# New order lists for five engines in a graph-network kernel of four layers

## The reference

```python
H = (adj != 0); w = adj[:, 0]                       # layer 0: hypergraph convolution, twice
h = relu(Dn * (H @ (Be * (H.T @ (x @ W1.T)))) + b1) # Dn, Be: reciprocals of row sums
x = ln(x + conv(ln0(h), W2) + b2 + x)
q, k = split(x @ Wqk); v = x @ Wv                   # layer 1: a softmax over the nodes
x = ln(x + softmax(sum(q * (adj @ k)) / 16) * v)
s = (Q @ K.T) * scale * 2 * adj                     # layer 2: attention, 8 heads of 32
x = ln(x + (softmax(s) @ V) @ Wo.T + bo)
xg = x * sigmoid(deg * Wd + bd)                     # layer 3: gated, scores times adj
QK = sigmoid(xg @ Wqk3.T + bqk); a = (QK @ QK.T) * adj
x = ln(x + relu((a / sum(a)) @ xg @ Wl.T + bl + xg @ Wr.T))
```

## Time and profile before

| | us |
|---|---|
| runs before (three), median | 960.44 |
| lowest and highest | 959.28, 968.0 |
| span of the profiled execution | 966.0 |
| busy: TensorE | 887.1 (92%) |
| busy: VectorE, ScalarE, GpSimd | 742.3, 724.6, 670.3 |

### The profile page before, as it was taken

The page is one execution under the profiler, slowest core; times in us unless marked ns, Lnnn a source line. Parts: engine busy times, 40 slices in busy tenths (PEclk is TensorE's granted clock), DMA queues, the critical chain, the costliest instruction groups (busy, mean ns, idle before and its releaser), DMA issues.

```text
span 966.0 us, 34322 instructions
## 1 busy us (share of the span) xinstructions
PE 887.1 (92%) x12124; PEld 761.5 (79%) x12124; DVE 742.3 (77%) x2292; ACT 724.6 (75%) x1740; POOL 670.3 (69%) x1005
## 2 busy tenths in 40 slices
PE   4778898999999999999999999999999999988674
PEld 3556677888888888888888888888888888876542
DVE  5556776888888888888888888888888888876632
ACT  3445567888888888888888888888888888867631
POOL 2575667777777787777777777877778777764421
PEclk9798899999999999999999999999999999999955
DMA  8002443444454444444344444443443444444320
GB/s 207 20 21 83 111 100 65 119 111 106 112 123 121 116 116 102 103 112 109 106 109 110 122 123 117 114 106 99 111 119 103 104 115 116 109 97 116 97 48 22
DMA packets 194573, 99.46 MB, mean 103 GB/s; under 512 B 112866, under 2 KB 194276, under 8 KB 194532
## 3 DMA queue, kind: packets, MB, share of 16 engines
q1 hardware_dynamic: 194532, 98.93, 40.6%
HBM read 48.28 MB, written 25.17 MB: 76 GB/s over the span
## 4 chain that ended last, share of the span: by engine, by line
PE 53%; ACT 11%; POOL 10%; DVE 10%; issue 9%; DMA 5%; SPq 1%; POOLq 0%; DVEq 0%; ACTq 0%
PE bank L537 12%; PE bank L539 12%; PE bank L538 12%; POOL rFl L1375 3%; PE bank L562 3%; ACT r L886 3%; PE bank L754 2%; PE bank L815 2%; DMA k_by_head<-kst 2%; DMA Ks<-k_by_head 2%; PE bank L650 1%; ACT x L846 1%; PE bank L682 1%; ACT rFh L826 1%; POOL rsC L1391 1%
## 5 line engine op out<-in xcount | busy, mean ns | idle before, releaser
L1375 POOL TENSOR_TENSOR rFl<-r,rFh 128x512 f16<-128x512 f32 x64 | 74.2, 1160 | 81.1 <-ACT rFh L826 81.1
L537 PE MATMUL bank<-z1h,W 128*128 128x256 f16 x256 | 71.9, 281 | 6.3 <-DVE z1l L1025 6.3
L538 PE MATMUL bank<-z1l,W 128*128 128x256 f16 x256 | 71.8, 281 | 0.0
L537 PE MATMUL bank<-W,rFh 128*128 128x256 f16 x256 | 71.8, 280 | 0.0
L539 PE MATMUL bank<-z1h,W 128*128 128x256 f16 x256 | 71.7, 280 | 0.0
L539 PE MATMUL bank<-W,rFl 128*128 128x256 f16 x256 | 71.7, 280 | 0.0
L538 PE MATMUL bank<-W,rFh 128*128 128x256 f16 x256 | 71.7, 280 | 0.0
L1476 POOL TENSOR_TENSOR late<-late,Smx 128x512 f32<-128x512 f32 x64 | 66.8, 1043 | 1.3 <-DVE Smx L1282 1.0
L1375 POOL TENSOR_TENSOR y0l<-y,y0h 128x512 f16<-128x512 f32 x32 | 37.3, 1166 | 42.3 <-ACT y0h L826 42.3
L870 ACT ACTIVATE Pf<-bank,Dinv 128x128 f32<-128x128 f32 x64 | 20.0, 363 | 49.7 <-DVE Dinv L1167 49.7
L886 ACT ACTIVATE r<-bank,b1c 128x256 f32<-128x256 f32 x128 | 50.1, 471 | 4.8 <-PE bank L539 4.8
(11 more groups left out here) (281 smaller groups left out, 4188.3 us busy)
## 6 DMA issues: line engine op xcount, KB each, us to landing
Qs<-q_by_head SPq DMA_DIRECT2D x96, 128.0 KB, 2.7
Ks<-k_by_head SPq DMA_DIRECT2D x96, 128.0 KB, 3.2
Vbd<-vst SPq DMA_DIRECT2D x128, 66.0 KB, 2.1
xin<-x SPq DMA_DIRECT2D x32, 256.0 KB, 2.8
q_by_head<-qst SPq DMA_DIRECT2D x32, 256.0 KB, 2.5
k_by_head<-kst SPq DMA_DIRECT2D x32, 256.0 KB, 2.1
out<-late SPq DMA_DIRECT2D x32, 256.0 KB, 2.9
aC<-adj_mask SPq DMA_DIRECT2D x32, 65.0 KB, 2.2
```

Source lines behind the costliest of these rows:

```text
L537: pe.matmul(o, sh, mh, start=start, stop=False, skip_group_check=True)
L538: pe.matmul(o, sh, ml, start=False, stop=False, skip_group_check=True)
L1375: return pool.tensor_tensor(dst, a, b, ALU.subtract)
```

## The change

All order lists (`ORDER`, `HEAD` and `TAIL` for TensorE, ScalarE, VectorE, GpSimd and SP) are replaced; a step holds the same pieces, and nothing else of the kernel differs. The lists were drawn up by a planner that now counts the changes between whole-array and 64-wide products. Two of the fifteen tables:

```diff
-ORDER_PE = [3, 2, 1, 5, 2, 4, 4, 2, 0, 3, 1, 0, 2, 0, 5, 4, 0, 0, 5, 3, 1, 3, 4, 5, 1, 2, 5, 5, 2, 0, 1, 0, 4]
+ORDER_PE = [1, 2, 3, 3, 5, 0, 2, 1, 5, 0, 4, 4, 2, 0, 2, 4, 0, 1, 5, 3, 3, 0, 4, 5, 2, 1, 5, 5, 1, 2, 0, 0, 4]
-ORDER_ACT = [0, 4, 3, 2, 1, 0, 0, 3, 5, 0, 5, 2, 5, 1, 4, 0, 0, 0, 0, 1, 2, 0, 4, 5, 0, 3, 2, 4, 3, 4, 1, 4, 2, 3, 3, 4, 5]
+ORDER_ACT = [4, 1, 0, 3, 5, 5, 0, 0, 2, 5, 0, 1, 3, 4, 4, 2, 1, 4, 2, 0, 0, 0, 0, 5, 0, 2, 0, 1, 3, 4, 3, 4, 3, 2, 4, 3, 5]
```

More of the change, by code:

```diff
@@ L61 @@
-TAIL_POOL = [[1, 1, 3, 4, 5, 1, 1, 1, 3, 1, 2, 2, 3, 4, 4, 4, 5, 5, 5], [4, 3, 5, 2, 2, 4, 4, 3, 3, 4, 5, 5, 5], [4, 5, 4, 4, 3, 4, 3, 5, 3, 5, 5], [4, 5, 4, 4, 4, 5, 5, 5], [5, 5, 5, 5]]
+ORDER_PE = [1, 2, 3, 3, 5, 0, 2, 1, 5, 0, 4, 4, 2, 0, 2, 4, 0, 1, 5, 3, 3, 0, 4, 5, 2, 1, 5, 5, 1, 2, 0, 0, 4]
+ORDER_SP = [4, 3, 3, 0, 3, 0, 3, 0, 5, 2, 3, 2, 2]
+HEAD_SP = [[0, 0, 0], [0, 0, 0], [0, 0, 2, 0, 2, 2], [3, 0, 3, 3, 0, 3, 3, 2, 0, 2, 2], [3, 3, 0, 4, 0, 0, 3, 2, 3, 3, 2, 2], [3, 0, 3, 3, 0, 0, 3, 4, 2, 5, 3, 2, 2]]
@@ new lines @@
+TAIL_SP = [[3, 3, 4, 3, 3, 2, 5, 3, 2, 2], [3, 5, 4, 3, 3, 3, 2, 3, 2, 2], [3, 5, 3, 4, 3, 3, 3], [4, 5], [5]]
+ORDER_ACT = [4, 1, 0, 3, 5, 5, 0, 0, 2, 5, 0, 1, 3, 4, 4, 2, 1, 4, 2, 0, 0, 0, 0, 5, 0, 2, 0, 1, 3, 4, 3, 4, 3, 2, 4, 3, 5]
+ORDER_DVE = [1, 0, 0, 0, 2, 0, 0, 0, 2, 0, 3, 0, 0, 1, 1, 1, 0, 4, 4, 2, 2, 4, 5, 4, 0, 5, 2, 4, 3, 3, 5, 3, 1, 5, 3, 5, 3, 5, 4, 2, 1, 3, 3, 5, 1, 0, 1, 5, 5, 0, 2, 0, 4, 3]
+ORDER_POOL = [0, 0, 1, 1, 0, 3, 0, 4, 1, 1, 1, 2, 2, 1, 5, 3, 0, 0, 0, 4, 0, 4, 3, 4, 5, 5, 0, 5, 0]
@@ new lines @@
+HEAD_PE = [[0, 0, 0, 0, 0, 6, 6, 6, 0, 0], [1, 0, 0, 0, 1, 0, 0, 6, 1, 1, 0, 1, 0], [2, 1, 2, 2, 0, 2, 0, 1, 0, 0, 0, 1, 2, 1, 2, 1, 0, 0], [1, 2, 3, 2, 2, 0, 1, 0, 2, 0, 3, 0, 3, 3, 0, 2, 1, 1, 2, 1, 0, 0], [2, 1, 4, 3, 4, 0, 2, 4, 1, 2, 0, 4, 0, 2, 3, 0, 0, 3, 1, 4, 3, 2, 1, 2, 1, 0, 0], [1, 3, 2, 3, 5, 1, 2, 4, 4, 0, 2, 5, 0, 2, 4, 0, 1, 3, 3, 5, 0, 0, 1, 5, 2, 4, 5, 5, 1, 2, 0, 0, 4]]
+HEAD_ACT = [[6, 0, 0, 0, 0, 0, 0, 0, 0, 0, 0], [6, 0, 6, 0, 0, 1, 0, 6, 6, 0, 0, 0, 1, 0, 0, 1, 0, 1], [0, 2, 1, 0, 0, 2, 0, 2, 1, 0, 0, 0, 1, 0, 0, 2, 0, 1, 2], [0, 6, 6, 1, 3, 2, 0, 6, 0, 6, 6, 0, 6, 2, 3, 0, 1, 2, 0, 0, 1, 0, 0, 2, 0, 3, 1, 3, 3, 3, 2], [4, 1, 3, 2, 0, 4, 0, 4, 0, 4, 4, 0, 4, 3, 2, 0, 1, 0, 0, 1, 2, 0, 0, 2, 0, 4, 1, 3, 2, 3, 3, 3], [4, 3, 1, 0, 3, 2, 5, 5, 0, 5, 0, 1, 0, 2, 1, 4, 2, 4, 0, 0, 0, 0, 5, 0, 1, 0, 2, 4, 4, 3, 3, 4, 3, 3, 2, 4, 5]]
@@ new lines @@
+HEAD_POOL = [[0, 0, 6, 0, 0, 0, 0, 0, 0, 0, 0], [0, 0, 0, 0, 1, 1, 1, 1, 1, 1, 6, 0, 0, 0, 0, 0, 0], [0, 6, 0, 0, 1, 1, 0, 6, 2, 2, 1, 1, 1, 1, 0, 0, 0, 0, 6, 0, 0], [0, 1, 0, 0, 1, 0, 3, 1, 1, 1, 1, 2, 2, 3, 3, 0, 0, 0, 0, 0, 0], [1, 0, 0, 0, 4, 1, 3, 0, 4, 4, 1, 1, 1, 2, 2, 4, 1, 0, 3, 0, 0, 0, 3, 0, 0], [4, 1, 1, 0, 0, 3, 0, 0, 1, 1, 1, 1, 2, 2, 5, 3, 0, 0, 0, 0, 4, 4, 3, 4, 5, 5, 0, 5, 0]]
+TAIL_PE = [[1, 3, 2, 5, 2, 4, 2, 1, 5, 3, 4, 5, 2, 4, 5, 3, 3, 4, 1, 5, 2, 5, 1, 2, 4, 1], [3, 3, 5, 2, 4, 2, 5, 2, 4, 5, 4, 2, 5, 4, 3, 3, 5, 2, 5, 2, 4], [3, 3, 4, 5, 4, 5, 4, 5, 4, 5, 3, 3, 5, 5, 4], [5, 5, 4, 4, 5, 4, 5, 4, 5, 5, 4], [5, 5, 5, 5, 5, 5]]
@@ new lines @@
+TAIL_ACT = [[1, 3, 2, 5, 4, 5, 5, 3, 4, 5, 2, 1, 4, 2, 4, 1, 4, 2, 3, 4, 1, 3, 2, 3, 4, 3, 5], [3, 4, 5, 5, 3, 2, 5, 4, 5, 4, 4, 2, 4, 2, 2, 3, 4, 3, 3, 2, 3, 4, 5], [3, 3, 5, 5, 4, 5, 4, 4, 4, 5, 4, 4, 3, 3, 4, 3, 3, 5], [5, 5, 4, 5, 4, 4, 4, 5, 4, 4, 4, 5], [5, 5, 5, 5, 5]]
+TAIL_DVE = [[1, 2, 2, 3, 1, 5, 1, 2, 4, 5, 2, 4, 1, 4, 4, 5, 5, 5, 3, 2, 4, 3, 3, 3, 5, 4, 3, 3, 1, 5, 2, 5, 5, 1, 3, 2, 4, 3, 1, 1], [2, 2, 3, 4, 5, 3, 4, 5, 4, 4, 2, 2, 5, 3, 5, 5, 4, 5, 2, 4, 3, 3, 3, 3, 2, 5, 3, 5, 2, 5, 3, 4], [4, 4, 3, 4, 3, 4, 5, 5, 4, 5, 5, 3, 5, 4, 5, 3, 3, 3, 3, 5, 5, 5, 3, 4, 3], [5, 4, 5, 4, 4, 4, 5, 5, 5, 4, 4, 5, 5, 5, 5, 4], [5, 5, 5, 5, 5, 5, 5, 5, 5]]
@@ L63 @@
+TAIL_POOL = [[1, 1, 3, 4, 5, 1, 1, 1, 2, 2, 1, 3, 4, 4, 4, 5, 3, 5, 5], [3, 4, 5, 2, 2, 4, 4, 3, 3, 4, 5, 5, 5], [3, 4, 5, 4, 4, 3, 4, 3, 5, 5, 5], [5, 4, 4, 4, 4, 5, 5, 5], [5, 5, 5, 5]]
 LAST_LAG = 5
```

13 lines of the change are left out of this document (1 added, 12 removed).

## The result

The changed kernel takes **1157.22 us** (median of four runs, 1154.01 to 1160.69), against 959.86 for the kernel before on the same chip: ratio 1.205, 95% interval 1.198 to 1.212. The profiled execution took 1157.87, its span is 1156.1. So the direction was forecast, and the size was not: 976.5 was forecast, 988 was the upper end.

The account below looks back on a forecast made before the run. A closed ring through all engines, 5.69 + 11.67 + 3.94 + 5.80 = 27.10 us a step against 26.48, was to bound the changed kernel; 26 x 0.62 = 16.1 added to 960.4 gave 976.5 us, range 953 to 988.

Parts of the forecast that it names:

- Elsewhere in a step I see no longer loop: VectorE's y, HT to HBl behind GpSimd's rsc: claimed to reach line 608 at about 27 us, an estimate with less certain rows.
- The rival for it: TensorE waits at line 608 for HBl: each 0.1 us costs 2.6; at 0.3 a step, 27.4 and 984; chance 0.12.
- nbB: GpSimd's pair of instructions ahead of x1: taken at the long 0.93 us; the short value, 0.52, gives a 26.69 step.
- The first leg: From line 608's products over VectorE and GpSimd to ScalarE's x1: 5.69 us, a gain of 1.44 from 7.13.
- x1 to veF: ScalarE's stretch from x1 to GpSimd's veF: 11.67 us, up from 10.10, with vst, uh and the norm of C inside.
- veF to the turn: GpSimd from veF over rsF and xg to TensorE's turn of xg: 3.94 us, with rsq's second sum now between.
- The turn to line 608: TensorE from turning xg to the next step's line 608: 5.80 us, as before.
- Line 798's wait: TensorE's transpose waiting for GpSimd's SAs: 0.32 us a step lost before; most or all of it was to go.
- A change of width: TensorE switching between whole-array and 64-wide products: still 0.20 start to start; four fewer at 0.09 save 0.36 us a step.
- TensorE idles at line 562: A sign: TensorE waiting there behind xg by some 0.6 us a step.
- At line 646: A sign: TensorE idle there behind rsq, sharing with line 562 some 1.3 us of waits a step.
- the ring: Closed loop of orders and data through all engines, one step long: 27.10 us a step, 0.62 above the old 26.48.

Follow-up runs that it names:

- GpSimd's list put back: The changed kernel with y behind wrm and VectorE's first low part of Ehl behind mvG, GpSimd's list as in the changed kernel: 1076.09 us, ratio 1.123.
- y back: The changed kernel with y alone moved back in VectorE's loop list to where it was before the change: 1017.64 us, ratio 1.056.
- the third try: The changed kernel with five fp32 products of 512 columns on TensorE ahead of its wait for HBl, in odd steps only: 1121.88 us, ratio 1.164.

## Why the prediction was right in direction and wrong in size

**The step that failed** is "Elsewhere in a step I see no longer loop": that y at the head puts HT to HBl behind rsc and reaches line 608 "at about the same 27 us". The places were read rightly: with GpSimd's rows short, that path adds 6.40 - 5.89 = 0.5 us to TensorE's own leg, about what rsc was stretched by (1.19 for 0.77); y waits for rsc there, but no run takes that stretch away alone. The lengths were not: no sum is shown for them, and in the rows of before, by which they come to 27, GpSimd ran none of its 1.2 us rows beside HT, HBh or HBl. In the new place they meet five of these, and y to HBl takes 6.99 instead of 3.08. The rival for it ("each 0.1 us ... at 0.3 a step") named the wait and its line, and was sized at 0.3 where 4.5 came.

The Trainium skill's page "SBUF — State Buffer", section "Who interferes with whom", holds the rule, and the prediction used it for nbB alone. It says that VectorE contends with a GpSimd instruction that reads SBUF if it has two inputs there itself, and with GpSimd if it runs a kind such as a tensor-scalar in its two-port mode, not if it has at most one input there outside that mode, and that one of the two is then blocked for a whole instruction. The runs agree row by row: HT, cnt and HBh (tensor-scalar) and HBl and Ehl (two inputs) are the long ones, y, ul and preG (a bank and one input from SBUF) and the reduce of line 1139 (0.42 in every run) are not. This holds in the steady stretch of all fourteen traces: HBl takes 1.18 to 1.35 where it begins beside a GpSimd row of over 0.9 us that has 0.2 us or more to go (the small powers left out), 0.34 to 0.35 where none is beside it; HT 1.07 to 1.08 and 0.28 to 0.30; y 0.46 to 0.49 in both cases. In which mode the tensor-scalars ran, no row shows.

**What the prediction didn't have** is the price of a long wait. The first leg was forecast at 5.69 and is 5.81 where line 608 hardly waits; behind 4.3 us of standing still it is 7.74. The run with products in the wait puts 2.0 of it on the granted clock. At half clock the path through z1h is also another than the one that was summed.

**What was right.** x1 to veF: 11.67 forecast, 11.65 to 11.68 in the kernel after and in all its variants but the one with GpSimd's list put back. veF to the turn: 3.94 forecast, 4.00 where rsF is not held; in the kernel after rsF's own stretch of 0.45 is the error, the same mechanism as for HBl. The turn to line 608: 5.80 forecast, 5.89 where TensorE alone sets it (y back). nbB: 0.93 forecast, 0.81 to 0.88 with GpSimd's rows short, where x1 does wait for it; and 0.50 in the kernel after, where Ql came later. Line 798's wait went. TensorE idles at line 562, by 1.02. At line 646, where a part of the idle time was forecast, there is next to none in the loop (1.8 us in all). A change of width still costs 0.20 to 0.21 from start to start, and the step from the final product to layer 1's scores, 64 rows to 128 rows, 0.21 as well (563.55 to 563.76), so three changes were saved and not four. That agrees with the Trainium skill's page "TensorEngine Tiling (Array Packing)", section "Tiling Modes", as the prediction has it. It can have made no difference to the time, since TensorE had more than that to wait. The direction came out as forecast, but only 0.62 of the 7.65 us a step that were lost are the ring's, for which it was forecast.

**The sum of the loss**, a step: the ring as forecast 0.62, HT to HBl 3.9, the clock 2.0, rsF 0.45, rsc 0.5, together 7.5 of some 7.65 measured; the rest is in the small misses of the legs.

**What holds the kernel before at 26.48.** The prediction took TensorE for the bound, with the ring 0.21 behind, and the wait at line 798 for a loss of TensorE's. TensorE's own work was cut by some 0.18 ahead of line 798 and the step did not move. In both kernels line 798 starts 12.33 behind line 608 (486.22 to 498.55; 480.02 to 492.35), and the next line 608 14.17 behind that. So the traces show another loop, which the prediction didn't have: from line 608 over x1 (7.12 to 7.13) to GpSimd's first rFl (3.62 later), SAs behind it (1.11) and line 798 (0.45), and from there TensorE without a wait to the next line 608. The run that drew the scores together takes SAs off this loop, but it ran into the wait for x1F; so no run shows what lies under it.

## What to carry to other kernels

The length of a VectorE or GpSimd row belongs to its place as much as to the operation. Whoever moves a row must look at what the other of the two does in the new place: if both read SBUF in the ways above, the row that comes second is to be priced up to the end of the neighbour and a little more (here 0.05 to 0.15), and a run of long neighbours without gaps holds each short row in turn.

A wait of several us on TensorE is to be priced with the slower clock that may stand behind it, here 2 us on top of 4.3. The length of the wait alone does not tell the price: behind 4.2 us the clock was 0.65 and not 0.50 in most of the steps without products of the third try, and behind 2.1 us it was 0.65 with Ehl's low part behind mvG, but 1.00 in four of five such steps with it behind preG.

## What the runs showed of the hardware that was not expected

- A VectorE row of 0.24 us (each of the two of HBh) took 1.10 and 1.19 beside GpSimd's additions and subtractions of 1.2, over four times as long; GpSimd's small powers (rsF, rsc: 128 x 2) went from 0.70 to 1.15 and 1.20 beside one VectorE row of 0.68 with two inputs. Either engine can be the one that is held.
- A shift of 0.3 to 0.4 us between the two engines can be enough: with wcl ahead of the bias of xin, or with rsc at 0.70 and y sooner behind it, the bias met HBh, HBl slipped beside y0l, and most steps grew by 0.3 to 2.0 us.
- With nine more fp32 products a step the loop's program seems to be fetched anew in each round of two steps (2.16 MB of instructions instead of 0.39), at some 3 to 3.8 us of standing still in nearly every round; with five products in every other step it is not.
